# Attention over a context: maximum units in pairs, quotients from the bank of sums, sums of probabilities over four key tiles

## The reference, cut to what matters

```
xn, yn = _ln(x, ...), _ln(y, ...)
q = einsum('bsc,hcd->bhsd', xn, wq);  k = einsum('btc,hcd->bhtd', yn, wk);  v = ...
a = softmax(einsum('bhsd,bhtd->bhst', q, k) * D ** (-0.5), axis=-1)
if causal: a = a * mask             # after the softmax; only a1
o = einsum('bhst,bhtd->bhsd', a, v)
x_out = x + o @ li1_w + li1_b
```

## Time and profile before

| | us |
|---|---|
| median of three runs | 8038.13 |
| profiled execution | 8022.59 |
| its span | 8020.8 |
| TensorE busy | 7135.1 |
| VectorE busy | 5918.4 |
| ScalarE busy | 4951.6 |
| GpSimd busy | 2313.2 |

### The profile page before, as it was taken

How to read it: one execution, slowest core, us unless ns; L and a number is a source line. 1 busy time by engine, 2 the same in 40 slices (tenths; PEclk the granted TensorE clock), 3 DMA queues, 4 the chain that set the end, 5 groups by cost and what they waited for, 6 DMA issues and landing times. The chain is left out here.

```text
span 8020.8 us, 186125 instructions
## 1 busy us (share of the span) xinstructions
PE 7135.1 (89%) x73814; PEld 3142.3 (39%) x73814; DVE 5918.4 (74%) x12885; ACT 4951.6 (62%) x9846; POOL 2313.2 (29%) x2368
## 2 busy tenths in 40 slices
PE   6999999878999997888599999999998779999979
PEld 2333333353333333444244444444444533333335
DVE  6888888657989996677466666666665469899855
ACT  4778887636888884444255555555554248888852
POOL 1222222111121110444245444544444211221200
PEclk9999999888999998788699999999999779999989
DMA  4444333114433421000100000000000144434400
GB/s 97 101 95 92 83 83 92 45 26 100 99 89 77 99 65 31 15 16 13 53 6 8 7 6 10 6 10 6 7 3 18 49 83 96 96 84 85 97 22 14
DMA packets 319828, 417.80 MB, mean 52 GB/s; under 512 B 56533, under 2 KB 238053, under 8 KB 318968
## 3 DMA queue, kind: packets, MB, share of 16 engines
q1 hardware_dynamic: 317432, 405.36, 22.4%
q10 hardware_dynamic: 1536, 0.53, 0.0%
HBM read 225.41 MB, written 174.66 MB: 50 GB/s over the span
## 5 line engine op out<-in xcount | busy, mean ns | idle before, releaser
L687 ACT ACTIVATE a_probs<-scores_ps 128x512 f32<-128x512 f32 (+2 forms) x5248 | 2821.7, 591 | 356.2 <-PE scores_ps L607 263.4
L746 DVE TENSOR_REDUCE a_unit_max<-bank 128x1 f32<-128x512 f32 x3072 | 2004.0, 684 | 182.0 <-PE bank L594 147.3
L624 PE MATMUL bank<-a_probs,a_v_sb 128*9 128x256 f32 (+1 forms) x20992 | 1614.1, 379 | 29.4 <-ACT a_out_sb L694 20.4
L1275 ACT ACTIVATE cross_probs<-scores_ps 128x512 f32<-128x512 f32 (+1 forms) x1792 | 869.4, 571 | 772.6 <-PE scores_ps L1172 772.6
L1357 DVE TENSOR_REDUCE cross_unit_max<-bank 128x1 f32<-128x512 f32 x1536 | 1006.5, 687 | 319.7 <-PE bank L1158 316.9
L607 PE MATMUL scores_ps<-a_stack 64*128 64x256 bf16 (+1 forms) x10496 | 1131.5, 275 | 61.6 <-ACT a_probs L687 55.8
L1441 POOL TENSOR_TENSOR cross_added<-cross_probs 128x1024 f32<-128x1024 f32 x384 | 902.4, 2350 | 944.6 <-PE bank L1205 868.8
L746 DVE TENSOR_REDUCE a_unit_max<-scores_ps 128x1 f32<-128x512 f32 x1536 | 1050.2, 684 | 162.1 <-PE scores_ps L594 144.6
L594 PE MATMUL bank<-a_stack 63*128 63x512 bf16 (+2 forms) x3413 | 1039.7, 372 | 8.1 <-DMA a_stack<-a_stack_dram 2.6
L607 PEld LDWEIGHTS scores_ps<-a_stack 64*128 64x128 bf16 (+1 forms) x10496 | 373.5, 96 | 991.9 <-ACT a_probs L687 832.8
L594 PE MATMUL scores_ps<-a_stack 63*128 63x512 bf16 (+2 forms) x1707 | 635.9, 373 | 50.8 <-DMA a_stack<-a_stack_dram 47.5
(11 more groups left out here) (421 smaller groups left out, 10119.5 us busy)
## 6 DMA issues: line engine op xcount, KB each, us to landing
a_stack_dram<-a_parts SPq DMA_DIRECT2D x288, 400.2 KB, 4.3
a_stack<-a_stack_dram SPq DMA_DIRECT2D x256, 348.2 KB, 8.0
a_stack<-a_stack_dram SPq DMA_DIRECT2D x128, 444.2 KB, 9.9
a_ctxT<-in_ctxT SPq DMA_DIRECT2D x48, 400.2 KB, 4.9
a_stack_dram<-a_parts SPq DMA_DIRECT2D x288, 64.0 KB, 2.7
a_stack_dram<-a_parts SPq DMA_DIRECT2D x96, 128.0 KB, 2.8
f_x<-x_after_dram SPq DMA_DIRECT2D x32, 256.0 KB, 3.6
x_after_dram<-a_res SPq DMA_DIRECT2D x48, 128.0 KB, 4.6
```

Source lines behind the costliest of these rows:

```text
L624: ins = pe.matmul(out_bank[32 * h:32 * h + V8, q0:TOK], v[0:n, e.t, 4 * e.g + h, :], A.probs[0:n, held, o + q0:o + TOK], start=(e.t == 0), ...
L687: act.activation(by_pair(A.probs[0:n, b, a * 512:(a + 1) * 512])[:, :, q0:TOK], by_pair(score_bank[(2 * e.i + a) % 3][0:n, :])[:, :, q0:TO ...
L746: ins = dve.tensor_reduce(unit_max[:, e.g % 2, qt, 2 * a + j, c:c + 1], bank[:, 0:e.s.chunks[c][1]], AX.X, ALU.max)
L1275: act.activation(probs[0:n, b, h, 0:m, :].rearrange("p m q -> p (m q)"), score_bank[h][0:n, 0:m * TOK], ACT.Exp, scale=scale).then_inc(S[" ...
```

## The change

All of it is in `heads32` and its schedule.

- Units go in pairs. Both matmuls of a pair are queued together, on heads 0 and 1 or 2 and 3, into the two banks, which are now one PSUM tensor `M2`; VectorE takes the maximum of both in one operation, and then both count as taken. Per quad there are fourteen pairs, at places given by the table `PAIRS32` (step relative to the quad's base, slot, first unit). The own-token stage has pairs in slots 0 and 2.
- The context stage has no take: reciprocal and product read `out_bank` itself, and the next quad's first pv waits for the product (`normed`).
- In the context stage the probabilities of a step with odd j are added to those of the step before on GpSimd, in place, and the even step has no sums; the step with j = 6 keeps its own.
- q, k, v, turn, ctx and the statistics move to other steps, nearly all to slot 1, and proj from step 3 to step 2. In the context stage a unit waits for the cast of q as well, and the load of the batch after next waits for the transposed context in place of the transposed tokens.

```diff
+PAIRS32 = ((-1, ((0, 0), (2, 2))), (0, ((0, 4), (2, 6))), (1, ((0, 8),)), (2, ((0, 10), (2, 12))), (3, ((0, 14), (2, 16))),
+           (4, ((0, 18), (2, 20))), (5, ((0, 24), (1, 26), (2, 22))))
+    def summed(self, j):
+        return self.own or j % 2 == 1 or j == len(self.pairs) - 1
+    def joined(self, j):
+        return not self.own and j % 2 == 1
+    def unit32(self, k, u):
+        head = k % 4 // 2 * 2 + u % 2
-                prepare(step, 0, not late, "unit", g=g, k=k, r=int(k == s.NU - 1))
+                prepare(step, 0, not late, "unit", g=g, k=k, part=k // 2 * 2, r=int(k == s.NU - 1))
-                put((4, 5, 11, 12, 12)[j], 1, "ln_stats", j=j)
-                put((14, 15, 16, 17, 18)[j], 2, "ln_apply", j=j)
-            put(12, 2, "ln_rstd")
+                put((0, 4, 5, 6, 6)[j], 1, "ln_stats", j=j)
+                put(8 + j, 2, "ln_apply", j=j)
+            put(6, 2, "ln_rstd")
+            put(15, 1, "ctx", j=0)
+            put(19, 2, "x_turned")
+            put(22, 1, "ctx", j=1)
-        for j, (i, slot) in enumerate(((4, 0), (8, 0), (8, 2), (11, 0), (15, 0), (15, 2), (22, 0))):
-            prepare(i, slot, True, "v", j=j)
+        for j, i in enumerate((3, 9, 10, 16, 17, 23, 24)):
+            prepare(i, 1, True, "v", j=j)
-            prepare(base - 3, 2, nxt, "q", g=g)
-            for c in range(2):
-                prepare(base - 2, 2 * c, nxt, "k", g=g, c=c)
-            prepare(base + 6, 0, nxt, "turn", g=g)
-        proj_at = (3, 2)
+            prepare(base - 3, 1, nxt, "k", g=g, c=0)
+            prepare(base - 2, 1, nxt, "q", g=g)
+            prepare(base, 1, nxt, "k", g=g, c=1)
+            prepare(base + 6, 1, nxt, "turn", g=g)
+        proj_at = (2, 2)
-                        pe.wait_ge(S["heads_out"], e.takes)
+                        pe.wait_ge(S["heads_out" if own else "normed"], e.takes)
-                        ins = dve.tensor_reduce(unit_max[:, e.g % 2, qt, h, c:c + 1], bank[:, 0:n], AX.X, ALU.max)
-                    ins.then_inc(S["max_taken"], 1)
+                    if e.k % 2:
+                            ins = dve.tensor_reduce(unit_max[:, e.g % 2, qt, pair, c], max_banks[:, :, 0:n], AX.X, ALU.max)
+                        ins.then_inc(S["max_taken"], 2)
-                    chain(dve.reciprocal(inv[:, :], out_sb[:, e.g % 2, TOK:2 * TOK]))
+                    heads = out_sb[:, e.g % 2, :] if own else out_bank
+                    chain(dve.reciprocal(inv[:, :], heads[:, TOK:2 * TOK]))
+                    if not own and e.adds:
+                        pool.wait_ge(S["added"], e.adds)
+                    if s.joined(e.j):
+                        pool.wait_ge(S["added"], e.adds + 1)
+                        pool.tensor_tensor(added[:, e.i % ADDS32, :, :], added[:, e.i % ADDS32, :, :],
+                                           added[:, (e.i - 1) % ADDS32, :, :], ALU.add).then_inc(S["added"], 1)
```

More of the change, by code:

```diff
@@ L901, in segment32 @@
             for j in range(LN_PIECES):
[L902 to L909 removed]
+                put((0, 4, 5, 6, 6)[j], 1, "ln_stats", j=j)
[6 more added lines that the diff above has]
+            prepare(i, 1, True, "v", j=j)
         for quad in range(1, QUADS + 1):
             g, base, nxt = quad % QUADS, per_quad * (quad - 1), quad == QUADS
[L912 to L919 removed]
+            prepare(base - 3, 1, nxt, "k", g=g, c=0)
+            prepare(base - 2, 1, nxt, "q", g=g)
+            prepare(base, 1, nxt, "k", g=g, c=1)
+            for rel, places in PAIRS32:
+                for part, first in places:
+                    for k in (first, first + 1):
+                        prepare(base + rel, 0, nxt, "unit", g=g, k=k, part=part, r=int(k == PAIRS32[-1][1][-1][1] + 1))
+            prepare(base + 6, 1, nxt, "turn", g=g)
+        proj_at = (2, 2)
     if with_tail:
@@ L928, in segment32 @@
             plan.append(Ev("scores", s=s, g=steps[i][0], j=steps[i][1], i=zero + i))
-        first = 1 if any(e.kind in "kv" and not s.own for e in at.get((i, 0), [])) else 2
-        plan += at.get((i, 0), []) + units[0:first]
+        by_part = [[e for e in units if e.part == part] for part in range(3)]
+        plan += at.get((i, 0), []) + by_part[0]
         pv = with_core and 0 <= k < n_steps - LAG32 or with_tail and -LAG32 <= k < 0
@@ L933, in segment32 @@
             plan.append(Ev("pv", s=s, g=steps[k][0], j=steps[k][1], i=zero + k))
-        plan += units[first:first + 1] + at.get((i, 1), [])
-        if pv:
+        plan += by_part[1] + at.get((i, 1), [])
+        if pv and s.summed(steps[k][1]):
             plan.append(Ev("sums", s=s, g=steps[k][0], j=steps[k][1], i=zero + k))
@@ L938, in segment32 @@
                 plan += [Ev("take", g=steps[k][0], i=zero + k), Ev("norm", g=steps[k][0], i=zero + k)]
-        plan += units[first + 1:]
+        plan += by_part[2]
         if with_core and i < n_steps:
@@ L960, in schedule32 @@
     plan = [e for cur in range(-2, BATCH + 1) for e in segment32(s, cur)]
-    n = u = casts = takes = 0
+    n = u = casts = takes = adds = sums = 0
     side, cast, rows, summed, added = {}, {}, {}, {}, {}
@@ L964, in schedule32 @@
         if e.kind == "begin":
-            e.after = side.get(("x_turned", 0, e.cur + 1))
+            e.after = side.get(("x_turned" if s.own else "ctx", 0, e.cur + 1))
         if e.kind == "ln4":
@@ L980, in schedule32 @@
         if e.kind == "unit":
-            h, qt, c = s.unit32(e.k)
+            h, qt, c = s.unit32(e.k, e.u)
             e.cast = cast[e.g, e.batch, "k", c // 2]
+            if not s.own:
+                e.cast = max(e.cast, cast[e.g, e.batch, "q", 0])
             e.last = e.r == 1
@@ L992, in schedule32 @@
             e.free = summed.get(e.i - ADDS32)
+            e.adds = adds
             if s.pairs[e.j][1] - s.pairs[e.j][0] == 2:
-                added[e.i] = len(added) + 1
+                adds += 1 + s.joined(e.j)
+                added[e.i] = adds
         if e.kind == "pv":
@@ L1276, in program_act @@
                                        ACT.Exp, scale=scale).then_inc(S["probs"], 1)
-                if e.kind == "take":
+                if e.kind == "take" and own:
                     act.wait_ge(S["sums"], e.summed)
@@ L2376, in program @@
         G.S4 = ctx.enter_context(nc.psum_tensor("scores_ps", [P, 2, 2, 512], F32))
-        G.bank = [ctx.enter_context(nc.psum_tensor(f"bank{i}", [P, 512], F32)) for i in range(4)]
+        G.M2 = ctx.enter_context(nc.psum_tensor("max_ps", [P, 2, 512], F32))
+        G.bank = [ctx.enter_context(nc.psum_tensor(f"bank{i}", [P, 512], F32)) for i in range(2)]
+        G.bank += [G.M2[:, 0, :], G.M2[:, 1, :]]
         sb = Mem(nc, ctx, "shared")
```

39 lines of the change are left out of this document (22 added, 17 removed).

## The result

The changed kernel takes 8102.3 us (median, 8098.1 to 8138.3) against 8034.8 for the kernel before on the same chip: ratio 1.0093, 95% interval 1.0061 to 1.0125. It is slower by 67 us, 0.8%; 7985 was forecast, and the measured time lies above the range of 7900 to 8075. The profiled execution took 8138 us, the slowest of the four, where the one of before took 8023; 18 of these 116 us lie behind the context stage's last exponential, nearly all of it stages that the change doesn't touch, so the two profiles overstate the loss.

A forecast was written before the change was run, and what follows sets the result against it. TensorE's queue was taken as the bound before, round trips between pairs after. From the profiled 8022.6 us, -34 (context stage) and -19 (own-token stage) gave 7969.6, or 7985 on the median 8038.1; range 7900 to 8075.

The forecast's parts named there:

- The failing step: Context stage: from one pair's start to the next use of either bank, a round was put at 1.80 us.
- the hand-over of 0.42: From a unit's matmul start to the start of its reduction on VectorE: 0.42 us, read from one unit.
- -34: Context stage's term: 134.1 us a batch against 136.3, over 15.5 batches, 34 us less.
- Rival (a): Dearer round trip: joint reduction and hand-over take over 1.22 us at 768 full-width reductions; 8039 to 8119 us; chance 0.12.
- The sign: The whole kernel was forecast to get faster, 7985 us against 8038.1, with a chance of 0.65 for faster.
- The path, round by round: Context stage, going from pair to pair by the larger of 1.80 us and TensorE's work: 133.8 a batch, 134.1 with extras.
- What goes: 109 + 82 us: TensorE's queue in the context stage: 109 us of sums and 82 us of units go, 191 if TensorE stayed the bound.
- Rival (b): Lost rotation of banks costs more than the sums give: 243 us of waits against 191 and 19, 8071 us; chance 0.08.
- The rule against the change: Skill advice to break instructions up and rotate PSUM banks; the merge does the contrary, its effect on time being rival (b).
- Quotients: Context stage, VectorE: reciprocal reading PSUM taken at 1.75 us, bounded by 1.3 and 2.2; next quad's values wait for the product.
- GpSimd: Context stage: 192 more adds of 2.35 us, 451 us in all, were taken to cost nothing; ends 0 and 451.
- Own-token stage, forecast -19: Transposition's wait grows, +14 us; the third unit's 33.0 us of waits go; together -19, ends +34 and -53.

The follow-up runs named there:

- e4: Kernel before with only the quotients read from the bank of sums, without ScalarE's copy: 7983 us, ratio 0.9922.
- e11: Kernel before with both the joined sums and the quotients read from the bank, single maxima in their old places: 7944 us, ratio 0.9886.
- e5: Changed kernel with single maxima, each with its own wait and each bank counted as taken by itself: 7794 us, ratio 0.9702.
- e9: Changed kernel with single maxima per bank, and the sums of every step back on TensorE: 7840 us, ratio 0.9757.
- e3: Kernel before with only the joined sums (second addition on GpSimd), ScalarE's copy kept: 8291 us, ratio 1.0321.
- e10: Changed kernel with single maxima per bank, and ScalarE's copy of the sums' bank put back: 7981 us, ratio 0.9936.
- e12: Changed kernel with single maxima per bank, and both ScalarE's copy and the sums of every step put back: 7871 us, ratio 0.9794.
- e2: Changed kernel with one wait for the joint maximum, and the pair's waits all on its first matmul, none on the second: 8041 us, ratio 1.0008.
- e1: Changed kernel with each joint maximum waiting for one semaphore, that of the pair's second matmul, in place of two: 8086 us, ratio 1.0067.
- e8: Changed kernel with one wait for the pair, then two single maxima, counted as taken together: 8082 us, ratio 1.0066.
- e6: Changed kernel with the sums of every step back on TensorE: 8080 us, ratio 1.0071.
- e7: Changed kernel with ScalarE's copy of the sums' bank put back ahead of the quotients: 8248 us, ratio 1.0263.

## Why the prediction was wrong

The sizes of the parts, put into the kernel before one after the other: quotients from the bank -52 (e4); joined sums -39 and -46 (e11 against e4, e5 against e9); pairs and their places, with the second halves of the projections in the pair's bank, -150 (e5 against e11); the joint maximum **+308** (the changed kernel against e5). The 150 are all that e5 still has of the change beside e11, the own-token stage too: 120 lie between the first and last exponential of the context stage, 25 between those of the own-token stage. The joined sums are a gain only beside quotients from the bank; beside ScalarE's copy they cost 256 us (e3) and 110 (e10 against e12).

1. **The failing step: "from one pair to the next use of either bank there are at least 0.42 + 1.22 + 0.15 = 1.79, with the second matmul's start 1.80 us."** 1.22 was measured as 1.226 and 0.15 as 0.146; the hand-over of 0.42 was 0.632. I took it from a single unit that found its bank free and added 0.01 for the second matmul. A pair has 0.554 even where it finds both banks free. One that was held back differs from the unit in three things: its second matmul, with waits of its own, starts 0.125 after the first (e2 takes that away), the reduction's second wait is 0.03 (e1), and an operation over two banks starts 0.07 later (e8). With 0.2 more, the 8 rounds a quad that bind by e1 and e2 give 64 x 8 x 0.2 = 102 us, which carries 7985 to 8087; measured 8102. The stage by itself fits less well: -34 + 102 = +68 was to be expected, and the profile has +94. Up to 15 of the 26 left can be the additions to the residual (36.1 us in all, 21.4 before), which the prediction didn't have; the rest is open. Rival (a) had the place and the kind of price, 768 reductions and hand-overs that cost more than 1.22; but its sizes were lengths of the reduction, and all of the excess lies in the hand-over.
2. **The sign.** The path, round by round, was the right picture: the forecast had 134.1 a batch at 1.80, and 4 x 8 x 0.2 more is 140.5, where 142.4 was measured. It left the forecast 0.7% below no change with a price that is paid 48 times a batch, and each 0.1 of a round is worth 50 us. That sensitivity stood nowhere in the range but in rival (a), at a chance of 0.12.
3. **What goes: 109 + 82 us.** TensorE's busy time fell by 123 of these. None of it showed in the time once the round trip bound (e6: no loss with the sums back). In e5, where it is on the path, sums give 46, not 109. Pairs and places give 120 in the context stage, more than the 82; TensorE's waits for maxima are 129 us in e11 there and 37 in e5, which fits, but the two weren't taken apart.
4. **Rival (b)**, the lost rotation, had the mechanism and the side right: the merge costs 308 us by e5, against waits of 3.8 us x 64 = 243 worked out there, and 8102 against its 8071. I gave it 0.08 because part of the waits seemed to be in the kernel before already. They were: TensorE waits 68 us for maxima there and 37 in e5, so other parts of the change take some of them away. And its 243 was worked out with rounds of 1.80. The rule against the change (the Trainium skill, Perfetto Trace Analysis, Optimizing Scalar/DVE Operations: where VectorE isn't saturated but causes bubbles elsewhere, breaking instructions up may let work finish sooner) is borne out by e5, which breaks them up again and is 3.8% faster, at 21 us more of VectorE. But e8 breaks them up too and gains nothing, so what counts here is that each bank is awaited and counted by itself.
5. **Quotients**: the row's 1.75 held (1.748), the values' wait for the product came (44.0 us at 54 places), and e4's -52 shows the edit to be a gain, which the prediction had not priced apart.
6. **GpSimd** at nothing: right for what was priced, 576 adds of 2.35 us and sums that waited once. What the adds do to VectorE's work from SBUF was not priced.
7. **Own-token stage, forecast -19**: both things that were named are there. The unit's waits of 33.0 us are 1.5, and the transposition waits 1.72 us where it waited 1.18. Rows of the changed kernel's waits (us, times, longest) and of TensorE:

```profile
PE bank L1235 <- DVE own_negmax L1381: 84.6, 52, 2.5
...
PE max_ps L1174 <- DVE own_unit_max L1374: 1.5, 3, 0.9
```

```profile
3602.89 0.41 PE L1235 MATMUL bank<-shared_ident,own_negmax 128*128 128x128 f32 x2 [1.72 <-DVE own_negmax L1381]
```

The stage is 559 us against 558. In e4, whose own-token stage is that of before, it was 574 at a clock of 0.80 in place of 0.83, so a change of 19 us can't be read from one profile of each. All the profiles together point the forecast's way: from first to last exponential the stage takes 556 to 574 us in the four kernels that have the stage of before (mean 566), 559, 531 and 561 in the changed kernel, e6 and e7, whose own-token stage is the same (mean 550), and 530 to 545 in the other seven, at clocks of 0.80 to 0.83 in the first four and 0.81 to 0.89 in the rest. So the term was about right in the mean, and a single execution can hide it.

## What to carry to other kernels

Before merging two operations that drain two PSUM banks, price the round trip, matmul to matmul, and ask whether the other engine has work that needs neither bank. Here two reductions of 0.69 with a count each beat one of 1.23 by 308 us, though VectorE did more. Read a hand-over from the same arrangement (as many matmuls, waits and banks, and held back), not from a single unit that found its bank free, and when a forecast hangs on a term taken hundreds of times, say what 0.1 us of it is worth. Measure the parts one by one and in pairs: three of this change's four parts were gains together, and without the fourth it is the fastest version (7794 us), but one of the three, the joined sums, costs 256 us in the kernel before by itself. Before giving GpSimd more adds, look for VectorE operations with both inputs in SBUF.

## What the runs showed of the hardware

- A second matmul with its own waits started 0.125 us after a held-back first; without waits 0.006 (e2). A second semaphore wait ahead of a reduction cost 0.03 (e1), a reduction over two banks in place of one 0.07 (e8). All are differences of medians over the pairs that waited for a maximum (299 in the changed kernel, 268 in e1, 257 in e2, 269 in e8).
- Two adds on VectorE with both inputs in SBUF take 0.59 us where they fall over the end of one GpSimd add and the start of the next, and 2.64 where they start just after one has started. e5 (VectorE, then GpSimd), then e10 (the same):

```profile
4497.12 0.59 DVE L1408 TENSOR_TENSOR cross_x_res<-cross_x_res,cross_b_out 128x128 f32<-128x128 f32 x2
```

```profile
4495.01 2.35 POOL L1470 TENSOR_TENSOR cross_added<-cross_added 128x1024 f32<-128x1024 f32 x1
4497.51 2.42 POOL L1466 TENSOR_TENSOR cross_added<-cross_probs 128x1024 f32<-128x1024 f32 x1
```

```profile
4542.22 2.64 DVE L1405 TENSOR_TENSOR cross_x_res<-cross_x_res,cross_b_out 128x128 f32<-128x128 f32 x2
4544.89 0.42 DVE L1408 TENSOR_TENSOR cross_res<-bank,cross_x_res 128x256 f32<-128x256 f32 x1
```

```profile
4542.20 2.51 POOL L1463 TENSOR_TENSOR cross_added<-cross_probs 128x1024 f32<-128x1024 f32 x1
```

  The VectorE adds of e10 end 0.15 us after GpSimd's add (4544.86 and 4544.71). The Trainium skill (SBUF — State Buffer, Who interferes with whom) says that a VectorE instruction with two SBUF inputs contends with a GpSimd one that reads SBUF, and that reductions don't: the trace agrees on the first, for these adds and for the products above, which with one input in PSUM keep their 0.42. The joint reductions keep their 1226 ns in a stage that GpSimd fills to 68%, but they read PSUM. These adds come once a batch, so by e10's row they cost at most 16 x 2.05 = 33 us.
- Less work for TensorE can come with less clock: e3 took sums away from it and gave adds to GpSimd, TensorE then waited up to 3.2 us for VectorE, and its granted clock over the stage went from 0.97 to 0.86.
